# Division of the softmax after the sum over values, in two of three attentions of a transformer block

## The reference

```python
attn = jax.nn.softmax(scores, axis=-1)          # exp(s - max) / sum(exp(s - max))
o = jnp.einsum('bnhqk,bnkhd->bnqhd', attn, v)
```

## Time and profile before

| | us |
|---|---|
| median of 2 runs | 1040.71 (1040.1 to 1041.33) |
| span of the profiled execution | 1041.6 |
| TensorE busy (matmul) | 852.6 (82%) |
| VectorE busy | 669.1 (64%) |
| ScalarE busy | 515.7 (50%) |
| GpSimd busy | 501.5 (48%) |

### The profile page before, as it was taken

How to read it: one execution, slowest core, us unless ns; L and a number is a source line. 1 busy time by engine, 2 the same in 40 slices (tenths; PEclk the granted TensorE clock), 3 DMA queues, 4 the chain that set the end, 5 groups by cost and what they waited for, 6 DMA issues and landing times.

```text
span 1041.6 us, 21054 instructions
## 1 busy us (share of the span) xinstructions
PE 852.6 (82%) x5919; PEld 616.2 (59%) x5919; DVE 669.1 (64%) x2576; ACT 515.7 (50%) x2068; POOL 501.5 (48%) x576
## 2 busy tenths in 40 slices
PE   4879677888889966898898968778898996788897
PEld 4556356666556645676664645656665664566664
DVE  2247888844536888874445689885444679887443
ACT  0257334455557543345565744444455763334555
POOL 3246645633335555453433565554433555555334
PEclk9789899999999988999998998999999998899999
DMA  8441000000100100000000000000000000000000
GB/s 268 123 142 30 18 25 13 18 20 16 31 19 18 30 21 17 21 16 19 24 13 22 27 17 25 15 20 22 16 22 26 12 11 11 11 6 7 1 6 16
DMA packets 33860, 31.15 MB, mean 30 GB/s; under 512 B 7613, under 2 KB 29363, under 8 KB 33475
## 3 DMA queue, kind: packets, MB, share of 16 engines
q1 hardware_dynamic: 33731, 29.66, 9.8%
HBM read 21.20 MB, written 2.15 MB: 22 GB/s over the span
## 4 chain that ended last, share of the span: by engine, by line
PE 47%; DVE 32%; issue 9%; ACT 3%; POOL 3%; SPq 3%; DMA 2%; DVEq 1%; POOLq 0%; ACTq 0%
PE dense_bank L897 9%; PE score_bank L939 9%; PE o_bank L957 6%; DVE left L646 6%; DVE left L657 6%; PE dense_bank L904 6%; PE turn_bank L926 5%; DVE top L640 4%; DVE top L652 4%; PE dense_bank L866 3%; PE dense_bank L875 3%; PE dense_bank L878 2%; PE dense_bank L884 2%; DVE ln_stats L677 2%; DVE x_mid L730 2%
## 5 line engine op out<-in xcount | busy, mean ns | idle before, releaser
L573 ACT ACTIVATE probs<-score_bank,neg_max 128x128 f32<-128x128 f32 x768 | 272.0, 371 | 230.6 <-DVEq L650 146.6
L939 PE MATMUL score_bank<-k_blocks,q_t 128*128 128x512 f32 x384 | 211.6, 640 | 11.3 <-issue 6.2
L567 ACT COPY probs_t<-turn_bank 128x512 f32<-128x512 f32 x192 | 112.7, 587 | 152.7 <-PE turn_bank L926 143.9
L957 PEld LDWEIGHTS o_bank<-probs_t,v_pad 128*32 128x32 f32 x1536 | 73.1, 111 | 163.0 <-issue 96.2
L484 POOL TENSOR_TENSOR probs<-probs,row_sum 128x512 f32<-128x512 f32 x128 | 133.0, 1046 | 72.6 <-DVE row_sum L783 72.1
L573 ACT ACTIVATION_READ_ACCUMULATOR probs<-score_bank,neg_max 128x1 f32 x768 | 160.4, 209 | 0.0
L435 POOL TENSOR_SCALAR ln_var<-ln_mv 128x1 f32<-128x1 f32 x80 | 15.2, 190 | 266.6 <-DVE ln_mv L680 264.9
L957 PE MATMUL o_bank<-probs_t,v_pad 128*32 128x128 f32 x1536 | 125.7, 284 | 19.5 <-issue 19.0
L897 PE MATMUL dense_bank<-h_t,w_m 128*128 128x128 f32 x1024 | 126.6, 282 | 14.2 <-DVEq L694 13.0
L897 PEld LDWEIGHTS dense_bank<-h_t,w_m 128*128 128x128 f32 x1024 | 120.0, 195 | 20.0 <-ACT h_t L533 7.0
L492 POOL TENSOR_SCALAR left<-left 128x512 f32<-128x512 f32 x64 | 95.5, 1492 | 69.0 <-DVE left L657 68.3
(11 more groups left out here) (110 smaller groups left out, 1442.5 us busy)
## 6 DMA issues: line engine op xcount, KB each, us to landing
k_blocks<-k_t SPq DMA_DIRECT2D x384, 16.0 KB, 1.8
gates<-gates_dram SPq DMA_DIRECT2D x16, 384.0 KB, 3.5
k_blocks<-in_L_xcond_w_ada SPq DMA_DIRECT2D x3, 768.0 KB, 9.4
x_in<-in_x SPq DMA_DIRECT2D x16, 128.0 KB, 2.1
ctx_in<-in_ctx SPq DMA_DIRECT2D x16, 128.0 KB, 2.4
w_m<-in_L_xcond_w_m SPq DMA_DIRECT2D x1, 2048.0 KB, 12.3
out_y<-x_mid SPq DMA_DIRECT2D x16, 128.0 KB, 1.7
w_m<-in_L_xcond_w_m SPq DMA_DIRECT2D x1, 1024.0 KB, 14.5
```

The costliest lines, as they stand in the source:

```text
L567: nc.scalar.copy(probs_t[:, u % 3].rearrange("p h t -> p (h t)"), turn_bank[u % TURN_BANKS][:]).then_inc(probs_t_ready, 1)
L573: e = nc.scalar.activation(probs[:, t % 4, h], score_bank[t % SCORE_BANKS][:, P * h:P * h + P], ACT.Exp, bias=neg_max[:, t % 4, h:h + 1], ...
L939: nc.tensor.matmul(score_bank[u % SCORE_BANKS][:], q_t[:, r, c], k_blocks[:, r, c, blk:blk + 4].rearrange("p h t -> p (h t)"), start=True, ...
L957: e = nc.tensor.matmul(o_view[lane:lane + 32, c, what], w, probs_t[:, u % 3, 2 * g + odd], start=(odd == 0), stop=(odd == 1))
```

## The change

In SELF and LAST, GpSimd no longer multiplies the probabilities. TensorE transposes the exponentials as they are and sums them over the values. The row sums of a phase (16 heads) are kept together; once a phase VectorE inverts them (128x16), GpSimd spreads each over its head's 16 channels (128x256, tokens on partitions), and a new dense part "inv" turns the result: two TensorE transposes into a dense bank, one ScalarE copy from there to inv_sum. VectorE's copy from o_bank to o_t becomes a product with inv_sum. The part "inv" stands at the seventh step of its phase (step 6 of 0 to 11 for SELF 0, 38 for LAST 0, and every four steps after: 6, 10, 14, 18 and 38, 42, 46, 50), as the first of its sequence's parts at that step. In plan order, step 18 is then kv LAST 0, kv CROSS 2, inv SELF 3, and step 38 is inv LAST 0, q LAST 2, up 3. GpSimd spreads two steps before. The spread tile lies in the same memory as inv_sum, so GpSimd and ScalarE wait for the product of the phase before. In CROSS the waits' numbers change and nothing else. bias_rows moves into a part of glu that is free during setup.

```diff
--- before.py
+++ after.py
@@ -75,7 +75,7 @@
-            (3, "skip", SELF), (8, "out", SELF), (9, "stats", CROSS), (10, "skip", CROSS), (11, "norm", CROSS),
+            (3, "skip", SELF), (6, "inv", SELF), (8, "out", SELF), (9, "stats", CROSS), (10, "skip", CROSS), (11, "norm", CROSS),
@@ -84,13 +84,13 @@
-            (14, "q", LAST), (24, "out", LAST)):
+            (14, "q", LAST), (22, "inv", LAST), (24, "out", LAST)):
-DENSE_USES = {"q": 1, "kv": 1, "turn": 1, "turn_ctx": 1, "out": 1, "up": 2}
+DENSE_USES = {"q": 1, "kv": 1, "turn": 1, "turn_ctx": 1, "out": 1, "up": 2, "inv": 1}
...
-        row_sum = sb("row_sum", P, 4, QH)
+        row_sum = sb("row_sum", P, 2, 4, QH)
+        inv_row = sb("inv_row", P, 2, H)
+        inv_wide = inv_sum[:].rearrange("p c (h d) -> p (c h) d", d=D)
...
@@ -477,13 +481,14 @@
-                    if 0 <= u < UNITS and u // (4 * SLOTS) != CROSS:
-
-                        n = u if u < 4 * SLOTS else u - 4 * SLOTS
-                        pool.wait_ge(inv_row_done, i * (UNITS - 4 * SLOTS) + n + 1)
-                        nc.gpsimd.tensor_tensor(probs[:, u % 4], probs[:, u % 4],
-                                                row_sum[:, u % 4].unsqueeze(2).broadcast_to([P, QH, P]),
-                                                ALU.mult).then_inc(weights_ready, 1)
+                    if 0 <= u < UNITS and u // (4 * SLOTS) != CROSS and u % 4 == 3:
+                        ph = u // 4
+                        m = ph if ph < SLOTS else ph - SLOTS
+                        pool.wait_ge(inv_row_done, i * 2 * SLOTS + m + 1)
+                        pool.wait_ge(o_t_ready, i * PHASES + ph)
+                        pool.sem_inc(pool_passed, 1)
+                        nc.gpsimd.tensor_copy(inv_wide, inv_row[:, ph % 2].unsqueeze(2).broadcast_to([P, H, D])
+                                              ).then_inc(inv_wide_done, 1)
@@ -538,6 +543,14 @@
+                if name == "inv":
+                    ph = phase_of(kind, s)
+                    act.wait_ge(o_t_ready, i * PHASES + ph)
+                    act.wait_ge(dense_ready, base + n + 1)
+                    nc.scalar.copy(inv_sum[:].rearrange("p c t -> p (c t)"),
+                                   dense_bank[n % DENSE_BANKS][:, 0:2 * P]).then_inc(inv_done, 1)
+                    act.wait_ge(inv_done, i * PHASES + kind * SLOTS + s + 1)
+                    act.sem_inc(dense_free[n % DENSE_BANKS], 1)
@@ -764,10 +777,8 @@
                         if ph // SLOTS == CROSS:
                             nc.vector.reciprocal(inv_sum[:], o_view[:, :, 1]).then_inc(inv_done, 1)
-                            dve.wait_ge(inv_done, i * SLOTS + ph % SLOTS + 1)
-                            nc.vector.tensor_tensor(o_t[:], o_view[:, :, 0], inv_sum[:], ALU.mult).then_inc(o_t_ready, 1)
-                        else:
-                            nc.vector.tensor_copy(o_t[:], o_view[:, :, 0]).then_inc(o_t_ready, 1)
+                        dve.wait_ge(inv_done, i * PHASES + ph + 1)
+                        nc.vector.tensor_tensor(o_t[:], o_view[:, :, 0], inv_sum[:], ALU.mult).then_inc(o_t_ready, 1)
@@ -778,9 +789,11 @@
-                    if 0 <= u < UNITS and u // (4 * SLOTS) != CROSS:
+                    if 0 <= u < UNITS and u // (4 * SLOTS) != CROSS and u % 4 == 3:
+                        ph = u // 4
+                        n = ph if ph < SLOTS else ph - SLOTS
                         dve.wait_ge(probs_ready, i * UNITS + u + 1)
-                        nc.vector.reciprocal(row_sum[:, u % 4], row_sum[:, u % 4]).then_inc(inv_row_done, 1)
+                        nc.vector.reciprocal(inv_row[:, ph % 2], row_sum[:, ph % 2].rearrange("p u h -> p (u h)")).then_inc(inv_row_done, 1)
@@ -897,6 +910,14 @@
+                if name == "inv":
+                    ph = phase_of(kind, s)
+                    m = ph if ph < SLOTS else ph - SLOTS
+                    pe.wait_ge(inv_wide_done, i * 2 * SLOTS + m + 1)
+                    for c in range(CK):
+                        wide_c = inv_wide[:, HC * c:HC * c + HC].rearrange("p h d -> p (h d)")
+                        e = nc.tensor.transpose(d[:, P * c:P * c + P], wide_c, ident[:])
+                    e.then_inc(dense_ready, 1)
@@ -917,8 +938,11 @@
-                        pe.wait_ge(weights_ready, i * UNITS + u + 1)
                         src = left if u // (4 * SLOTS) == CROSS else probs
+                        if u // (4 * SLOTS) == CROSS:
+                            pe.wait_ge(weights_ready, i * 4 * SLOTS + u - 4 * SLOTS + 1)
+                        else:
+                            pe.wait_ge(probs_ready, i * UNITS + u + 1)
```

More of the change, by code:

```diff
@@ L166, in block_kernel @@
         b_out = sb("b_out", P, 4, C)
-        bias_rows = sb("bias_rows", NBIAS, P)
         bias_cols = sb("bias_cols", P, NBIAS)
@@ L210, in block_kernel @@
         glu = sb("glu", P, HB, P)
+        bias_rows = glu[0:NBIAS, HB - 1, :]
         gate_rows = glu[0:B].rearrange("p j t -> p (j t)")[:, 0:3 * C]
@@ L290, in block_kernel @@
         inv_row_done = sem("inv_row_done")
+        inv_wide_done = sem("inv_wide_done")
         weights_ready = sem("weights_ready")
@@ L574, in body @@
                                                      ACT.Exp, bias=neg_max[:, t % 4, h:h + 1],
-                                                     accum_out=row_sum[:, t % 4, h:h + 1])
+                                                     accum_out=row_sum[:, t // 4 % 2, t % 4, h:h + 1])
                         e.then_inc(probs_ready, 1)
@@ L810, in _ @@
             pe.wait_ge(rows_loaded, 9 * 16)
-            nc.tensor.transpose(dense_bank[0][:, 0:NBIAS], bias_rows[:], ident[0:NBIAS, 0:NBIAS]).then_inc(setup_pe, 1)
+            nc.tensor.transpose(dense_bank[0][:, 0:NBIAS], bias_rows, ident[0:NBIAS, 0:NBIAS]).then_inc(setup_pe, 1)
             pe.wait_ge(setup_dve, 2)
```

## The result

The changed kernel takes 1066.47 us (median of 2 runs, 1065.31 to 1067.64) against 1040.71 (1040.1 to 1041.33): the ratio is 1.025, with a 95% interval of 1.022 to 1.028. It is slower by 2.5%, though 118 us of GpSimd's work are gone. The forecast was 1057.5 within 1043 to 1068, so the range held the time, by 1.5 us at its upper end. The forecast itself was 9 us low, and the likeliest case was "no change" (0.72; "slower" had 0.25).

A forecast was written before the change was run, and what follows sets the result against it. TensorE bounds windowed attention, VectorE top-k, a chain of waits the last stretch. 1041.6 + 12.8 (step 18) + 6.0 (step 38) - 2.0 (first pass) = 1058.4, less 0.9 to the median: 1057.5 us, range 1043 to 1068.

The forecast's parts named there:

- Step 18: Top-k stretch: inv waits for kv LAST 0's bank, delaying scores and sums, so VectorE idles; 3.2 us a pass, +12.8 us.
- Step 38: Up projection waits for ScalarE's new copy, +2.2 us, less 0.7 from x_norm at step 37; +1.5 a pass, +6.0 us.
- The third rival: Last stretch: clock falls to half at the up projection, 3.4 us a pass, 13.6 in all, 1071 us; chance 0.16.
- Span and median: Whole kernel: profiled span stands 0.9 us above the median of the runs, so 1058.4 becomes 1057.5 us.
- Step 33: Normalisation before the last stretch's MLP: the prediction had no term here, forecast 0 for 34-36.
- x_norm under no division takes 0.4 us: Sign of being right: x_norm, up to 1.27 us before, takes 0.4 us where no division runs beside it.
- First pass: Steps near 6, behind the gates' DMA: of a 5.5 us wait for the multiplication, 2 us (0 to 5.5) returns.
- the sign that I had given for a late spread copy: Sign of being wrong: inv transposes seen waiting for GpSimd would mean the spread copy is late or slow.
- Step 42: Next pass's turn waits for the ScalarE copy, +0.65 us in two passes; up to 1.2 from the clock may return; net 0.
- Step 46: The 1.8 us wait goes, ScalarE starts 0.5 sooner and has 0.4 more work; 0.
- Costs taken at bounds: Added work: spread copy 0.6 us, product into o_t same as the 0.42 us copy, 16-column reciprocal 0.17 to 0.4; all 0.

The follow-up runs named there:

- e1: Changed kernel with inv put ahead of the two kv parts at step 18, nothing else different; 1053.27 us, 1.010 of the kernel before.
- e4: Kernel before, division kept, plus one blank dense-bank use (two transposes, one ScalarE copy) a pass at steps 18 and 38; 1064.05 us, ratio 1.021.
- a1: The changed kernel itself, unaltered, timed and profiled once more as a base; 1065.54 us, 1.023 of the kernel before.
- e9: Changed kernel, inv first at step 18 and last at 38, GpSimd's MLP and LAST skip parts waiting for the step's last normalisation; 1040.87 us, 0.9985 of before.
- e10: Changed kernel with the division moved in SELF only, inv first at step 18, LAST keeping its multiplications and reciprocals; 1042.47 us, 1.001 of before.
- e8: Changed kernel, inv first at step 18 and last at 38, skip parts of MLP and LAST one plan step later; 1051.07 us, 1.010 of before.

## Why the prediction was right or wrong

The direction, the two main places and their mechanism were right, and they make up 17 to 19 of the 25.8 us. That the time lay inside the range is in part owed to its width. What was missing is a term of 3.1 us at step 33, 2 us that the first pass did not give back, some 2 us at steps 42 to 46 and the end of a pass, and 3.9 us of difference between the profiled executions and the medians.

**Step 18: right.** 12.8 us forecast, 12.0 measured. The wait is in the named place (9.7 us at the inv transposes), o_t waits 3.45 us for the sums, and the clock is at half in between, which was the choice that made it 3.2 and not 1.4 a pass. e1 takes it away and e4 makes it without the change.

**Step 38: right, with the size nearly so.** Plain lengths give +1.7 us a pass (14.3 against 12.6) where +1.5 was forecast. The two parts of that term show singly: e4 has 2.4 us for the bank alone (2.2 forecast), and x_norm gives 0.66 back (0.7). Over four passes it is +5.2 in this profile, since two passes of before had half-clock spells of 0.7 and 0.9 us.

**The third rival, half the clock at the up projection, was not an alternative but an addition.** It does not fall in every pass: in the profile above in none, in a1 in two, at 1.7 us each (I had 3.4). That adds 3.3 us to a1's span and is most of the distance between the two profiled spans, 1063.5 and 1068.0. The sign that I had named for it, a mean clock below 0.9 in the last stretch, could not have shown it: a1's second pass, with the up projection at half clock, has 0.98 from 457 to 549 us.

**Span and median.** I took 0.9 us off the span of before to come to the median, which amounts to adding the 16.8 us to the median of before. The profiled execution that I had read was itself a long one, by some 2.7 us, with half-clock spells at steps 38 and 42 that are no part of the plain lengths.

**Step 33: missed.** The term that the sum puts at nothing is +3.1 us here: 0.4 a pass plain, 0.7 in the last, and 1.3 more with the clock in one. The prediction took x_norm to gain wherever a multiplication had stood beside it, and never asked where GpSimd's later work would go once it no longer waited for row sums. "x_norm under no division takes 0.4 us" holds at step 37 (0.46) and fails at step 33 (0.80) and at step 2 (0.81, again beside a skip part, where it had been 1.27). All 80 of them sum to 44 us instead of 57.6, and yet the path is longer, since the one that grew is on it. The Trainium skill ("SBUF — State Buffer", SBUF: two separate sides) says that whichever starts first, a GpSimd operation or a VectorE operation in a mode that uses two ports, has the shared port pair for the whole instruction, and the other blocks. No run here shows in which mode x_norm runs. By that the 0.72 us of the skip part, from 478.15, would end x_norm at 478.87 + 0.38 = 479.25; its row ends it at 479.01. The trace agrees in kind, with less than the whole, and in one place not at all: beside GpSimd's 1.49 us for the top-k, begun just before it, x_norm is through long before GpSimd is.

```profile
371.92 1.49 POOL L497 TENSOR_SCALAR left<-left 128x512 f32<-128x512 f32 x1 [0.50 <-DVE left L670]
371.96 0.71 DVE L698 TENSOR_SCALAR x_norm<-ctx_in,ln_mv,ln_rstd 128x256 f32<-128x256 f32 x1
```

**First pass: wrong.** I gave 2 us for the gates' DMA no longer blocking the transposes; 0-16 rose by 0.2. What I described did happen: the scores of unit 7 start at 60.2 instead of 67.5 us. Then the lead is lost at the next two:

```profile
62.31 0.72 POOL L458 TENSOR_TENSOR x_skip<-b_out,gates 128x256 f32<-128x256 f32 x1 [12.99 <-DMA gates<-gates_dram]
...
64.78 0.46 DVE L698 TENSOR_SCALAR x_norm<-x_in,ln_mv,ln_rstd 128x256 f32<-128x256 f32 x1 [5.69 <-POOL ln_rstd L442]
...
65.14 0.44 PE L919 MATMUL dense_bank<-ident,inv_sum 128*128 128x128 f32 x2 [3.35 <-POOL inv_sum L490]
...
68.31 2.07 PE L963 MATMUL score_bank<-k_blocks,q_t 128*128 128x512 f32 x2 [2.05 <-DMA k_blocks<-k_t]
```

The skip part still blocks GpSimd's power for the norm, and with it x_norm, the k/v projection and the k blocks' DMA: unit 8 leads by 3.3 us, unit 9 by 1.1, and 0.7 of that was there at the first score. The inv transposes wait for GpSimd as well, 3.35 us, the only time in the run: the sign that I had given for a late spread copy, though what held GpSimd up was the gates' DMA. I had named x_norm's wait until 65.6 and still paid out 2 us. Whatever does not pass GpSimd was free to run ahead, but the next scores do pass it.

**Step 42: the term of the ScalarE copy was right, its rebate was not.** 42-46 is 16.7 instead of 16.0 us in plain passes (+0.7, +0.65 forecast), in three passes instead of two, and the clock's 1.2 us did not come back in the second pass (18.4 against 17.6): +1.5 over all, with 0.7 won in the last pass.

**Step 46: right.** The wait of 1.8 us is gone and 46-next is 19.5 against 19.4 in the second pass; the +0.7 over all stand mostly in the last pass (14.7 against 14.2), which I did not follow up. The scores of unit 47 start 2 us after those of unit 46 instead of 3.9, but the k/v projection behind them begins 6.80 us after the scores of unit 46, against 6.79 before: exponentials, then the added copy, then h_t in ScalarE's queue.

```profile
552.15 0.42 ACT L550 COPY inv_sum<-dense_bank 128x256 f32<-128x256 f32 x1
...
552.83 0.81 ACT L538 ACTIVATE h_t<-dense_bank,mod_now 128x128 f32<-128x128 f32 x2 [0.26 <-ACT inv_sum L550]
553.69 1.16 PE L888 MATMUL dense_bank<-h_t,w_qkv 128*128 128x128 f32 x8 [1.60 <-ACT h_t L538]
```

**Costs taken at bounds.** The product into o_t takes 0.42 us, as the copy did. The spread copy takes 0.40 us (0.6 taken), the reciprocal of 16 columns 0.25.

**Open.** Why the clock falls in one pass and not in another with the same waits is not settled. A route for the inverted sums that needs no dense bank was not tried. The one other part with a price that the table does not explain is SELF in e9 and e10 (1.1 and 2.3 us more than before, in single profiles).

## What to carry to other kernels

Buffers taken by turns tie every user to the one before last: before adding a user, write the new order of takers out and ask who empties that buffer and what is queued behind the waiter; here the place within one step of the plan was worth 20 of 25 us. Work taken from an engine that is not the bound returns only its wait on the path, and the engine arrives earlier at whatever it does next: look for what that will overlap. A later slot in a queue's plan changes what stands before what, and delays nothing by itself; only a wait does.

## What was not expected of the hardware

- A VectorE normalisation of 128x256 in float32 takes 0.38 to 0.42 us alone, 0.46 when a GpSimd copy of 0.40 us begins just before it, 0.80 beside a GpSimd operation of 0.72 us, and 1.12 beside a multiplication of 1.04 us (step 37). In these last three it ends 0.14 to 0.15 us after the GpSimd operation. Beside GpSimd's 1.49 us for the top-k it takes 0.71 and ends first. A VectorE product of 128x512 went from 0.69 to 1.73 us beside a GpSimd product of 1.27 (e8).
- TensorE's clock comes as whole spells at half, each worth 0.7 to 1.7 us where TensorE's own queue sets the pace, and nothing where the next matmul waits for ScalarE anyway (38-40 of the changed kernel). Identical code has them in other places from one execution to the next: at the up projection in none or two of four passes, in two profiles of the changed kernel.
